# Self-attention outputs kept transposed through DRAM and projected directly, with the ternary weights' transposes at the head of the last part

## The reference, cut to what matters

```python
x = x + L0_xattn(layernorm(x), ctx, ...)    # cross attention, SELF ATTENTION, gelu feed-forward
x = x + L0_ffn(layernorm(x), ...)           # 8 experts, the best 2 of each token
x = x + L1_xattn(layernorm(x), ctx, ...)    # cross attention with prefix keys
x = x + L1_ffn(layernorm(x), ...)           # ternary weights
# self attention inside L0_xattn: 16 heads of 16, 1024 keys
probs = softmax(q @ k.T / 4); sa = (probs @ v) for each head, heads side by side
x = layernorm(sa @ so_w + so_b + x) * so_g + so_be
h = x @ fi_w + fi_b; inter = gelu(h); x = layernorm(inter @ fo_w + fo_b + x) * fo_g + fo_be
# L1_ffn: tern = clip(round(w / mean|w|), -1, 1); relu(x @ (tern_fc * scale).T + low rank)**2 @ (tern_proj * scale).T
```

## Time and profile before

| | us |
|---|---|
| median of 3 runs | 1101.11 |
| lowest, highest | 1099.83, 1109.42 |
| the profiled execution | 1096.52 |
| its span, first to last instruction | 1094.8 |
| mean granted TensorE clock in it | 0.975 |

### The profile page before, as it was taken

The page is one execution under the profiler, slowest core; times in us unless marked ns, Lnnn a source line. Parts: engine busy times, 40 slices in busy tenths (PEclk is TensorE's granted clock), DMA queues, the critical chain, the costliest instruction groups (busy, mean ns, idle before and its releaser), DMA issues.

```text
span 1094.8 us, 20748 instructions
## 1 busy us (share of the span) xinstructions
PE 1019.2 (93%) x7648; PEld 601.0 (55%) x7648; DVE 782.0 (71%) x1337; ACT 607.7 (56%) x1191; POOL 331.8 (30%) x724
## 2 busy tenths in 40 slices
PE   5999989999999999999988898989898999999998
PEld 3675666433333333333344665648677676576865
DVE  4786577689999999999723747546536756887565
ACT  2665554478888888888853123131222456556543
POOL 3422111001010343344103334373366433530000
PEclk9999999889999999999998997999999999999999
DMA  7302221451221212212125100021344301100000
GB/s 213 70 16 88 87 68 66 144 188 44 75 71 48 70 49 69 79 45 70 47 67 191 34 15 10 20 77 44 101 155 132 100 31 49 44 25 1 16 18 26
DMA packets 97578, 75.67 MB, mean 69 GB/s; under 512 B 49806, under 2 KB 87483, under 8 KB 97223
## 3 DMA queue, kind: packets, MB, share of 16 engines
q1 hardware_dynamic: 94407, 65.95, 20.0%
q0 software_dynamic: 3072, 8.39, 2.4%
HBM read 42.94 MB, written 30.93 MB: 67 GB/s over the span
## 4 chain that ended last, share of the span: by engine, by line
PE 65%; DVE 10%; DMA 8%; issue 5%; POOL 4%; ACT 4%; SPq 3%; POOLq 0%; DVEq 0%; ACTq 0%
PE OUT L855 15%; PE TR L855 14%; PE OUT L1090 9%; PE TR L861 8%; PE TR L1079 7%; DMA head_q<-MT 7%; PE OUT L1079 3%; PE TR L931 3%; PE SCR L915 2%; POOL dispatched L2038 2%; SPq L697 2%; ACT PTS L1298 2%; PE SCR L908 2%; DVE small L1486 1%; PE OUT L861 1%
## 5 line engine op out<-in xcount | busy, mean ns | idle before, releaser
L1555 DVE TENSOR_REDUCE small<-SCR 128x1 f32<-128x1024 f32 x256 | 308.5, 1223 | 26.2 <-PE SCR L962 20.3
L1396 ACT ACTIVATE shared<-TR 128x512 f32<-128x512 f32 x352 | 200.1, 597 | 38.8 <-PE TR L1079 30.7
L962 PE MATMUL SCR<-head_k,head_q 48*128 48x512 f32 x512 | 193.9, 456 | 2.7 <-DVE P L1531 2.7
L1090 PE MATMUL OUT<-shared,HM 128*32 128x256 f32 x2048 | 165.3, 394 | 1.2 <-ACT shared L1396 0.4
L1079 PE MATMUL TR<-head_q,head_k 51*128 51x512 f32 x352 | 149.7, 463 | 0.9 <-issue 0.6
L1919 POOL TENSOR_SCALAR small<-small 128x1 f32<-128x1 f32 x112 | 27.7, 247 | 346.7 <-DVE small L1487 344.5
L855 PE MATMUL TR<-xT,fifo 128*128 128x512 f32 x224 | 105.8, 629 | 1.1 <-ACT xT L1276 1.0
L1396 ACT ACTIVATE shared<-OUT 128x512 f32<-128x512 f32 x160 | 95.8, 599 | 19.3 <-PE OUT L1079 17.6
L1079 PEld LDWEIGHTS TR<-head_q,head_k 51*128 51x128 f32 x352 | 60.6, 186 | 76.4 <-ACT shared L1396 56.5
L1276 ACT ACTIVATE xT<-TR 128x256 f32<-128x256 f32 x96 | 35.4, 381 | 111.5 <-PE TR L861 108.6
L1090 PEld LDWEIGHTS OUT<-shared,HM 128*32 128x32 f32 x2048 | 41.4, 108 | 93.1 <-ACT shared L1396 57.6
(11 more groups left out here) (241 smaller groups left out, 1860.3 us busy)
## 6 DMA issues: line engine op xcount, KB each, us to landing
pieces<-pieces SPq DMA_DIRECT2D x16, 512.0 KB, 2.7
HM<-dispatched SPq DMA_DIRECT2D x46, 128.0 KB
expert_out<-HM SPq DMA_DIRECT2D x46, 128.0 KB
dispatched<-HB SPq DMA_DIRECT2D x6, 768.0 KB, 4.0
head_q<-pieces SPq DMA_DIRECT2D x32, 128.0 KB
head_k<-pieces SPq DMA_DIRECT2D x32, 128.0 KB
shared<-in_L_ffn_w SPq DMA_DIRECT2D x4, 1024.0 KB, 12.0
x<-TOK SPq DMA_DIRECT2D x16, 128.0 KB, 1.7
```

What stands on the lines that cost most here:

```text
L962: ins = nc.tensor.matmul(SQ[kt % 2][:, hf, :], QX[n % 2][rows, kt * 128:(kt + 1) * 128], KX[n % 2][rows, hf * 512:(hf + 1) * 512], start=T ...
L1090: ins = nc.tensor.matmul(PV[32 * g:32 * g + 32, 0:256], VH[:, n % 2, kt, :], PTB[:, kt % 2, g * 256:(g + 1) * 256], start=(kt == 0), stop= ...
L1396: nc.scalar.activation(PTB[:, kt % 2, hf * 512:(hf + 1) * 512], ring_bank("t_scores", n, kt, hf), ACT.Exp, scale=DH ** -0.5).then_inc(st_d ...
L1555: nc.vector.tensor_reduce(nm[:, n % 2, kt:kt + 1], SQ[kt % 2].rearrange("p h n -> p (h n)"), AX, ALU.max, negate=True).then_inc(sq_done.se ...
```

## The change

A head's output is no longer transposed. ACT copies `PV` into one of two halves of `OSB`, and SP stores 17 rows for each of the four groups (16 outputs and the sums), each row 1 KB, into `o_dram` of [32 heads, 17, 1024]. The sums of a batch are loaded as one 128x128 tile, DVE takes their reciprocals, and they go back to DRAM as `rs_dram`. For a block of four token tiles, the outputs `OT` (already feature by token) and the reciprocals repeated 16 times, `RT`, are loaded, 1 MB in four DMAs, and DVE multiplies them. `SO.t` then takes `OT` as it stands, so `ST` falls away. The loads for blocks 0 and 1 and the residual rows of the first tiles are issued inside part b, in passes 24, 25 and 26. The weights' transposes become steps `WF`, `WP`, `WS` that stand first in `ORDER_C`, with banks taken in turn, and the whole of `ORDER_C` is a new order. `TN` (POOL's scratch) moves from `OSB` to `HM`. Cut to its core:

```diff
-ST.0 ST.1 VW.0 RS.0 RS.1 SO.0 RS.3 SO.1 SN.0 RS.2 ST.2 ST.3 SO.3 SN.1 SO.2 LX.0 SN.3 LX.1 ST.4 RF.1 LD.5 LX.3 ST.5
-LD.7 RF.3 LD.4 ST.6 SN.2 LX.2 RF.0 RS.4 FI.0 RS.7 RS.5 LD.6 FO.1 SO.5 RS.6 FN.1 OL.2 FO.0 SO.4 SN.5 ST.9 SN.4 RF.2
...
-RT.5 FM.7 RS.13 FM.6 SN.11 SN.10 LD.15 LD.14 L2.7 LX.9 RT.7 RT.4 LX.11 ST.12 RF.9 RF.11 L2.6 RS.14 RS.15 RS.12 LX.10
-RT.6 GT.0 FI.2 RK.0 RF.10 FO.9 DS.7 SO.13 FN.9 FO.8 DS.0 SO.12 FN.8 DS.1 FO.10 SN.12 SN.13 FO.11 SO.14 SO.15 FM.9 DS.4
-DS.2 LX.12 LX.13 RF.13 SN.14 DS.3 SN.15 FM.8 L2.9 FN.10 RT.9 LX.14 LX.15 DS.5 FM.10 DS.6 FN.11 XL.3 FM.11 XL.1 XL.0
-L2.8 FI.3 RF.12 RT.8 RF.14 L2.10 XT.0 XL.2 RF.15 FO.13 UP.0 XT.1 FN.13 FO.12 UP.1 L2.11 FN.12 FO.15 XT.2 RT.10 HT.0
...
+WF.0 WF.1 WP.0 WP.1 WF.2 WF.3 WP.2 WP.3 WS RS.0 RS.2 RS.3 RS.1 SO.0 SO.1 SO.3 SO.2 SN.3 LD.6 SN.2 LD.5 SN.0 LD.7 SN.1
+RC LX.3 LX.0 RF.3 LX.2 LX.1 LD.4 OL.2 RF.2 FI.0 RS.5 RS.4 ON.2 RF.1 FO.1 SO.5 RF.0 FN.1 FO.0 RS.6 RS.7 SO.4 FN.0 SN.4
...
+L2.3 RT.2 RS.11 FO.7 FM.5 SO.9 FM.6 L2.4 LD.14 RT.3 RT.4 L2.5 L2.6 LX.8 FN.7 SO.11 FM.7 RS.12 LD.13 RT.5 SN.10 RT.6
+L2.7 RT.7 SN.9 LX.10 GT.0 SN.11 RK.0 DS.5 DS.3 DS.6 OL.3 RF.8 DS.1 ON.3 LX.9 DS.0 DS.4 LX.11 DS.7 DS.2 FI.2 XL.3 FO.8
+RF.10 SO.12 RS.14 RS.13 XL.0 FN.8 SN.12 RF.9 XL.1 FM.8 FO.9 LD.15 FO.10 SO.14 XT.0 XL.2 SO.13 RF.11 XT.1 RS.15 UP.0
+XL.5 XL.4 FN.9 SN.13 XT.2 UP.1 L2.8 FO.11 LX.12 HT.0 UP.2 LX.13 SN.14 SO.15 XT.3 DN.0 HT.1 LX.14 UP.3 SN.15 XT.4 HT.2
...
+        OT = PTS[:, :, :].rearrange("p h n -> p (h n)").rearrange("p (r k n) -> p r k n", r=2, k=KD)
+        RT = MW[:, :, :].rearrange("p r d -> p (r d)").rearrange("p (r k n) -> p r k n", r=2, k=KD)
...
-                    sp.wait_ge(aux_done.sem, taken["out", n])
-                    sp.dma_start(o_dram[:, :, n * DH:(n + 1) * DH], OH[:, n % 2, :, :]).then_inc(d_oh[n % 2], 16)
+                    sp.wait_ge(pv_done.sem, pv_done.base["b"] + n + 1)
+                    for g in range(4):
+                        sp.dma_start(o_dram[n, :, g * 256:(g + 1) * 256],
+                                     OSB[32 * g:32 * g + VW, n % 2 * 256:(n % 2 + 1) * 256]).then_inc(d_oh[n % 2], 16)
+
+                def load_sums(b):
+
+                    for r in range(2):
+                        sp.wait_ge(d_oh[r], DC + 64 * (b + 1) * H // 2)
+                    sp.dma_start(CA[:, b * 128:(b + 1) * 128],
+                                 o_dram[b * H:(b + 1) * H, DH, :].rearrange("h (c n) -> h c n", n=128)).then_inc(d_sums, 16)
...
+                def load_outputs(k):
+
+                    sp.wait_ge(d_rs, 16 * (k // BLOCKS + 1))
+                    c = slice(k % BLOCKS * N, (k % BLOCKS + 1) * N)
+                    for f in range(KD):
+                        h = slice(k // BLOCKS * H + f * (H // KD), k // BLOCKS * H + (f + 1) * (H // KD))
+                        sp.dma_start(OT[:, k % 2, f, :], o_dram[h, 0:DH, c]).then_inc(d_o[k], 16)
+                        sp.dma_start(RT[:, k % 2, f, :], rs_dram[h, c].unsqueeze(1).to_broadcast([H // KD, DH, N]))\
+                            .then_inc(d_o[k], 16)
...
+                    if n == 18:
+                        load_sums(0)
+                    if n == 22:
+                        store_reciprocals(0)
+                    if n == 24:
+                        sp.wait_ge(sums_ready, 1)
+                        load_outputs(0)
+                    if n == 25:
+                        load_outputs(1)
+                    if n == 26:
+                        for t in range(BT):
+                            load_residual(t)
...
-                    if kt == 5 and n >= 1:
-                        head_out_transposes(n - 1)
...
+                def fast_weights(i):
+                    k, hf = divmod(i, 2)
+                    transposes(out_bank(tl), [wfc[:, 4 * hf + c, k * 128:(k + 1) * 128] for c in range(4)])\
+                        .then_inc(out_full.sem, 1)
...
                 def self_projection(t):
-                    at.copied("ST", t)
-                    at.token_major(xTs, so, t, range(KD))
+                    pe.wait_ge(on_ready, t // BT + 1)
+                    at.token_major(OT[:, t // BT % 2], so, t, range(KD))
...
-                nc.scalar.activation(OSB[:, 0:256], PV[:, 0:256], ACT.Copy).then_inc(pv_done.sem, 1)
+                act.wait_ge(d_oh[n % 2], DC + 64 * (n // 2))
+                nc.scalar.activation(OSB[:, n % 2 * 256:(n % 2 + 1) * 256], PV[:, 0:256], ACT.Copy).then_inc(pv_done.sem, 1)
...
+            def reciprocals(b):
+
+                dve.wait_ge(d_sums, 16 * (b + 1))
+                sums = CA[:, b * 128:(b + 1) * 128]
+                nc.vector.reciprocal(sums, sums).then_inc(rs_ready, 1)
+
+            def outputs_norm(k):
+
+                dve.wait_ge(d_o[k], 16 * 2 * KD)
+                nc.vector.tensor_tensor(OT[:, k % 2], OT[:, k % 2], RT[:, k % 2], ALU.mult).then_inc(on_ready, 1)
...
-                    if kt == 6 and n >= 1:
-                        head_out(n - 1)
+                    if (n, kt) == (20, 4):
+                        reciprocals(0)
...
-            head_out(NH - 1)
             tl.close(sq_full, sq_done)
+            for k in range(BLOCKS):
+                outputs_norm(k)
```

More of the change, by code:

```diff
@@ L97 @@
     "OL": dict(),
-    "ST": dict(tr=1),
+    "RC": dict(),
+    "ON": dict(),
+    "WF": dict(out=1),
+    "WP": dict(tr=1),
+    "WS": dict(out=1),
     "RS": dict(res=1),
@@ L154 @@
[L154 to L158, removed]
@@ L268, in schedule_c @@
         before(("DS", t), ("FC", 0))
-        before(("ST", t), ("T", 0))
+        before(("SO", t), ("T", 0))
+        if k >= BLOCKS:
+            before(("ON", k), ("SO", t))
+            before(("SO", t - TB), ("OL", k))
     for i in range(2, B * NS):
@@ L274, in schedule_c @@
         before(("FI", k), ("L3", 0))
+    for k in range(BLOCKS, T // BT):
+        before(("RC",), ("OL", k))
+        before(("OL", k), ("ON", k))
+        before(("ON", k), ("UP", 0))
+    before(("ON", BLOCKS), ("ON", BLOCKS + 1))
+    for i in range(2 * KD):
+        before(("WS",), ("L2", i))
+        for t in range(BT):
+            before(("WF", i), ("LX", t))
+        for t in range(TB):
+            before(("WP", i), ("FM", t))
+            before(("WS",), ("L2", t))
     before(("RK", 0), ("GT", 1))
@@ L624, in build @@
                     emptied_at[ring[-1]] = (st_done.sem, st_done.base["b"] + (n * QT_PER_HEAD + kt) * 2 + hf + 1)
-                for kind, m, behind in (("max", n + 1, 2), ("out", n - 1, 5)):
-                    if kt == behind and 0 <= m < NH:
-                        ring.append((kind, m))
-                        emptied_at[ring[-1]] = (aux_done.sem, taken[kind, m])
-        ring.append(("out", NH - 1))
+                if kt == 2 and n + 1 < NH:
+                    ring.append(("max", n + 1))
+                    emptied_at[ring[-1]] = (aux_done.sem, taken["max", n + 1])
         slots = {item: i for i, item in enumerate(ring)}
@@ L1100, in maxima_transpose @@
                     .then_inc(aux_full.sem, 1)
-            def head_out_transposes(n):
-                pe.wait_ge(pv_done.sem, pv_done.base["b"] + n + 1)
-                transposes(free_bank("out", n), [OSB[:, s * 128:(s + 1) * 128] for s in range(2)]).then_inc(aux_full.sem, 1)
             pe.wait_ge(tr_done.sem, tr_done.base["b0"])
@@ L1701, in _ @@
             ins.then_inc(diag_ready, 1)
-            tl = Tally("w")
-            for k in range(KD):
-                for hf in range(2):
-                    bank = filled(tl)
-                    dst = fcT[:, k, hf * 512:(hf + 1) * 512]
-                    nc.vector.tensor_tensor(dst, dst, bank, ALU.add).then_inc(out_done.sem, 1)
-            nc.vector.tensor_copy(pscale[:, :], filled(tl)[:, 0:D]).then_inc(out_done.sem, 1)
             dve.wait_ge(d_zero, 16 * NH // 4)
```

162 lines of the change are left out of this document (73 added, 89 removed).

## The result

The changed kernel takes 1105.4 us (median of 20 runs, 1095.6 to 1113.7), the kernel before 1098.9 (median of 20). The ratio is 1.0053, 95% interval 1.0031 to 1.0074: slower by half a per cent. The profiled execution took 1106.28 us, its span is 1104.5, against 1096.52 and 1094.8 before.

What follows compares the result with a forecast made beforehand. It took most heads of part b as bound by a loop of DMAs, part c by PE with gaps. Part b +9.5 and part c -9.6 on the median 1101.1 gave 1101.0, stated as 1100, range 1084 to 1116.

Steps and rivals of the forecast that it cites:

- the clock's term: Part b: PE idles behind the output loads and drops to 1.2 GHz, +2 us (0 to 5).
- (3): Part b: output loads in passes 24 and 25 make the next heads late by 3.3 and 5.5, +8.8 us (0 to 12).
- (1): Part b: removing each head's transposes saves little because most heads wait for DMA, -3.3 us.
- (2): Part b: the store's 17-row DMAs use one engine, delaying only six heads with zeros, +2 us (0 to 4).
- upper bound of 12.6: Part b: the gain from removing the transposes if the landing moved along, -12.6 us.
- The start of part c: Last head's output to first gelu matmul: shorter than 21.75 us, taken as 17.1, -4.6 us (-2 to -6).
- the end of part b: The last head's output frees PE at 563.42 instead of 564.66, 1.2 us gained.
- ST and the new order: Rest of part c: twelve `ST` fewer, -2 us (-1 to -4); new order fills PE gaps, -3 (-8 to +6).
- (B): Rival, part b: new DMAs spread over all engines or one has room, all -12.9 us, 1088; chance 0.2.
- (C): Rival, part b: the store's engine overflows in every head, +21 to +40 us, 1121 to 1140; chance 0.1.
- (D): Rival, part c: PE waits 4 to 6 us before `RK.0`, gaps remain, +4 instead of -3, 1107; chance 0.14.
- (E): Rival, part b: landings move along with PE, the full -12.6 us and no delays, 1079; chance 0.06.

Runs made afterwards that it cites:

- late loads: The changed kernel with output loads moved from passes 24 and 25 to 29 and 30, residual rows from 26 to 31: 1087.3 us, ratio 0.9891.
- wide head loads: Query and key loads cut into DMAs of 16 rows: on the kernel before 1093.8 us, on the changed kernel 1081.5, on it with late loads 1073.3.
- old order: The changed kernel with late loads and, after the weights, part c in the order of the kernel before, without `ST`: 1091.6 us, ratio 0.9955.
- gelu before ranks: The changed kernel with `FI.2` ahead of `RK.0`, and `SN.11`, `LX.9`, `LX.11` ahead of both: 1112.7 us, ratio 1.0128.
- half loads: The changed kernel with each block's output loads halved, in passes 24, 26, 28 and 30, residual rows in 31: 1090.0 us, ratio 0.9936.

## Why the prediction went wrong

It said no change, 1100 us; the kernel is slower by 0.5%, inside the range. Its mechanism for the loss was right and its price too low.

- **The step that failed is the clock's term in (3).** It stood at 2 us, bounds 0 and 5. The runs show more by each way of counting. In the profiled executions PE needs 12.3 us more for the same matmuls of part b than with late loads. In the mean spans the loads cost 16.5 us; the two late heads are 15.02 - 10.7 = 4.3 and 16.75 - 10.7 = 6.0, together 10.3, where the sum had 3.3 + 5.5 = 8.8, and 6.2 are left over. Those are chiefly the two heads behind, which wait for nothing and take 6.7 and 1.4 us over their periods of 10.7 and 10.5, at clocks of 0.50 and 0.76. The two ways differ because a late head that runs slowly would otherwise have waited longer for its `MT`.
- **Its own row had a higher price.** The term was set beside a gap of 4.00 us in part c, in a stretch of 60 us with a mean clock of 0.89. That mean is 13.2 us at 1.2 GHz, and up to 6.6 us lost if PE is busy in them. Around the gap of the kernel before:

```profile
668.00:686.00 18.00, 13.72 (x40) 8.53 (x41) 12.12 (x41) 6.50 (x11) 8.42 (x14) 0.62 0.06 15
```

PE is busy 13.7 of these 18 us, the gap takes most of the rest, and 13.7 us run at 1.2 GHz. Two gaps follow each other in the changed kernel, and after the second PE stays at 1.2 GHz for 23.9 us, fully busy.
- **The ratio of the mended sum is partly luck.** With loads and clock at 16.5 instead of 10.8, the sum gives 1102.1 against the profiled 1096.5: 1.005, the ratio that was measured. But other terms are off and cancel: without the loads, part b gains 4.3 us where (1) and (2) had 1.3, and part c gains 6.8 to 8.0 where the sum had 9.6.
- **The size of the loads** was about 1.5 us short. 64 rows of 2 KB on each of eight engines were taken at 79 ns a row, 5.1 us; the load of pass 24 is issued from 485.56 on, and moves in most of this:

```profile
486.80:493.60 6.80, 6.28 (x63) 2.25 (x61) 5.84 (x6) 5.68 (x13) 4.22 (x10) 1.00 0.56 166
```

That is some 6.8 us, 8 from the first issue. The landings that the forecast gave for the next heads, 14.0 and 16.2 us after their predecessors' start, were 14.2 and 16.75.
- **The transposes** (1): right. 24 ordinary heads keep 10.75 us (10.79 before), the last three lose 0.37 each. The upper bound of 12.6 was real as well: wide head loads free 11.2 of it.
- **The store** (2): one engine carries it, as taken, and it hurts no ordinary head. In the six heads with zeros the 2 us do not show: none of the first 24 periods is over 11.2, and before there was one of 11.5. With the output loads behind it, its split gains 6.5 us. The gain of 1.1% with late loads (12 us, interval 8 to 16) against the sum without loads and clock, 3.3 - 2 + 9.6 = 10.9, says that everything else was sized well in sum.
- **The start of part c**: -5.7 instead of -4.6, and the end of part b -0.9 instead of -1.2.
- **ST and the new order**: -1.4 instead of -5. The old order without `ST` gives -1.6 from `FI.0` on, so the term of 2 for `ST` holds; the new order's 3 do not. It does not fill the gaps it was to fill: PE is busy 88.8 us in the same stretch, 89.0 before. Its one gain found is 1 us at the start.
- **Rivals.** (B), loads and store at no cost, gave -12.9 us; late loads give -12.0: the mechanism, had the loads been placed so. (C) is out. (D) was half right: the wait of 4 to 6 us before `RK.0` came as 5.95, but the order costs nothing in sum. (E) needs the wide head loads.

The rule of the Trainium skill, DMA: Bandwidth & Descriptors, "Why a DMA increments its semaphore by 16 and not by 1", is borne out in its counts, for 17 and for 8; which engines they are no row shows by itself, only that head loads wait behind them. The changed kernel's store alone on the queues, then an output load behind the end of a store (the last columns are the DMA share and GB/s):

```profile
402.50:404.50 2.00, 1.33 (x14) 0.55 (x14) 1.04 (x2) 0.97 (x3) 0.79 (x4) 1.00 0.07 24
```

```profile
490.60:492.00 1.40, 1.40 (x20) 0.55 (x13) 1.30 (x2) 1.18 (x4) 1.16 (x3) 1.00 0.47 167
```

One engine of sixteen is a share of 0.0625, eight are 0.5. The section "Specifications" of the same page of the Trainium skill, by which rows of 1 KB beat pieces of 64 bytes, bore on nothing here: in neither profile does an engine wait for a store.

**What stays open.** How much of the loads' 16.5 us is the clock's and how much is delay differs between executions: the changed kernel's mean clocks run from 0.952 to 0.966. The same part b in gelu before ranks was 337.9 us, with waits of 4.18 and 1.30 us, 6.4 us more PE time than with late loads, and heads 27 and 28 at 10.87 and 10.51, where the changed kernel's was 348.9. What decides whether the second wait is long, and how long the lower clock lasts, was not tried; nor was the share of the residual rows.

## What to carry to other kernels

A prefetch that is "hidden" must be costed on the engines that carry the loop's own loads, in the pass in which it is issued: the leading dimension of each DMA says how many they are. Put it where no load of the loop stands behind it, or cut it until it fits the slack. Where PE waits for a loop of DMAs, taking work from PE gains nothing until the loop is widened: here the transposes' removal, with all that goes with it, took 2 to 4 us off part b (332.4 to 330.7 and 328.0) with the narrow load, and 11 with the wide one. And a gap costs more than its length: look in a trace for how long the clock stayed low behind a gap like it (here 3 to 24 us), and count up to half of that.

## What the runs showed of the hardware

- After two waits of 4.0 us PE ran a whole head of 17.37 us, busy without a gap, at 1.2 GHz. In half loads, where no wait for `MT` is over 1.5 us, the granted clock of part b is 1.00.
- 64 rows of 2 KB on each of eight engines, with other traffic beside them, moved in about 6.8 us. In 1.4 us of it the share was 0.47 at 167 GB/s, 21 GB/s an engine; the 4 KB rows had 26.
- The 17 rows of 1 KB of each group all go through one engine: a share of 0.07 and 24 GB/s.
